# Non-local attention on one core: the first projections leave ScalarE ahead of the exponential's table, g and the result's shift go behind the first scores

## What is computed

```python
g     = (einsum('bchw,oc->bhwo', x, w_g) + b_g).reshape(B, N, Ci)
theta = (einsum('bchw,oc->bhwo', x, w_theta) + b_theta).reshape(B, N, Ci)
phi   = (einsum('bchw,oc->bohw', x, w_phi) + b_phi[:, None, None]).reshape(B, Ci, N)
att   = softmax(einsum('bnc,bcm->bnm', theta, phi), axis=-1)
y     = einsum('bnm,bmc->bnc', att, g).reshape(B, H, W, Ci)
out   = einsum('bhwc,oc->bohw', y, w_out) + b_out[:, None, None]
inv   = bn_gamma / sqrt(bn_var + BN_EPS)
out   = out * inv[:, None, None] + (bn_beta - bn_mean * inv)[:, None, None]
return x + out
```

## Time and profile before

| | us |
|---|---|
| median of three runs | 212.36 |
| lowest, highest | 211.96, 212.52 |
| the profiled execution: device time | 212.18 |
| its span, first to last instruction | 210.40 |
| TensorE busy (94% of the span) | 198.5 |
| VectorE busy (85%) | 178.4 |
| GpSimd busy (72%) | 152.4 |
| ScalarE busy (65%) | 136.8 |

### The profile page before, as it was taken

How to read it: one execution, slowest core, us unless ns; L and a number is a source line. 1 busy time by engine, 2 the same in 40 slices (tenths; PEclk the granted TensorE clock), 3 DMA queues, 4 the chain that set the end, 5 groups by cost and what they waited for, 6 DMA issues and landing times.

```text
span 210.4 us, 3966 instructions
## 1 busy us (share of the span) xinstructions
PE 198.5 (94%) x1100; PEld 130.9 (62%) x1100; DVE 178.4 (85%) x291; ACT 136.8 (65%) x245; POOL 152.4 (72%) x127
## 2 busy tenths in 40 slices
PE   7996989999999998999999999999999998999993
PEld 6585856586565856577555955667565854566542
DVE  0789899978998799978999599978999699989871
ACT  2776866758575847767577666756578575658721
POOL 2448898699669998699778998699887964774400
PEclk9999999999999999999999999999999999999999
DMA  5215967999999998899959995899977997786111
GB/s 156 88 60 154 212 126 155 229 215 168 230 106 247 229 183 167 165 249 232 189 129 259 220 200 133 190 252 216 153 160 167 224 170 166 134 108 114 50 37 66
DMA packets 59500, 35.28 MB, mean 168 GB/s; under 512 B 50400, under 2 KB 50912, under 8 KB 59488
## 3 DMA queue, kind: packets, MB, share of 16 engines
q1 hardware_dynamic: 59200, 35.01, 81.2%
q10 hardware_dynamic: 288, 0.14, 0.2%
HBM read 8.36 MB, written 4.23 MB: 60 GB/s over the span
## 4 chain that ended last, share of the span: by engine, by line
PE 58%; DVE 15%; ACT 12%; issue 10%; DMA 2%; ACTq 1%; DVEq 0%
PE ps_scores L721 17%; PE ps_y L733 11%; PE ps_flip L786 9%; ACT probs L544 8%; PE ps_misc L705 6%; DVE neg_max L586 6%; DVE pt_lo L686 5%; PE ps_y L740 5%; ACT pt_hi L532 4%; PE ps_misc L747 3%; PE ps_misc L811 3%; DVE y_norm L603 2%; PE ps_scores L759 2%; DMA w_tp<-w_tp_t_dram 2%; PE ps_flip L705 1%
## 5 line engine op out<-in xcount | busy, mean ns | idle before, releaser
L544 ACT ACTIVATE probs<-ps_scores,neg_max 128x1024 f32<-128x1024 f32 x64 | 71.7, 1120 | 32.3 <-DVE neg_max L591 23.4
L586 DVE TENSOR_REDUCE neg_max<-ps_scores 128x1 f32<-128x1024 f32 x64 | 77.8, 1216 | 0.9 <-PE ps_scores L721 0.9
L686 DVE SCALAR_TENSOR_TENSOR pt_lo<-ps_flip,pt_hi 128x512 f16<-128x512 f32 x84 | 54.0, 685 | 15.8 <-ACT pt_hi L532 15.6
L532 ACT ACTIVATE pt_hi<-ps_flip 128x512 f16<-128x512 f32 x84 | 45.7, 596 | 20.4 <-PE ps_flip L786 20.1
L721 PE MATMUL ps_scores<-phi_hh,theta_hl 128*128 128x512 f32 x128 | 45.8, 439 | 5.2 <-ACT probs L544 4.8
L426 POOL TENSOR_TENSOR p_lo<-probs,p_hi 128x1024 f16<-128x1024 f32 x22 | 47.1, 2141 | 4.3 <-POOL p_hi L422 2.6
L786 PE MATMUL ps_flip<-ident,probs 128*128 128x128 f32 x336 | 45.0, 276 | 1.0 <-ACT probs L544 0.6
L786 PEld LDWEIGHTS ps_flip<-ident,probs 128*128 128x128 f32 x336 | 37.2, 142 | 11.6 <-issue 5.7
L721 PE MATMUL ps_scores<-phi_ll,theta_hl 128*128 128x512 f32 x128 | 40.1, 394 | 0.0
L422 POOL TENSOR_SCALAR p_hi<-probs 128x1024 f16<-128x1024 f32 x22 | 23.6, 1071 | 11.3 <-ACT probs L544 8.3
L721 PEld LDWEIGHTS ps_scores<-phi_hh,theta_hl 128*128 128x128 f32 x128 | 19.3, 190 | 18.9 <-ACT probs L544 17.5
(11 more groups left out here) (80 smaller groups left out, 176.8 us busy)
## 6 DMA issues: line engine op xcount, KB each, us to landing
x_in<-x_in_dram SPq DMA_DIRECT2D x16, 256.0 KB, 3.3
inv_all<-inv_row SPq DMA_DIRECT2D x15, 256.0 KB, 4.1
out_dram<-resid SPq DMA_DIRECT2D x15, 256.0 KB, 2.7
phi_hh<-hi SPq DMA_DIRECT2D x14, 256.0 KB, 5.2
phi_ll<-lo SPq DMA_DIRECT2D x14, 256.0 KB, 5.7
theta_hl<-hi SPq DMA_DIRECT2D x7, 256.0 KB, 4.3
theta_hl<-lo SPq DMA_DIRECT2D x7, 256.0 KB, 5.1
pt_hi<-p_hi SPq DMA_TRANSPOSE x22, 4.5
```

What stands on the lines that cost most here:

```text
L532: nc.scalar.activation(pt_hi[ring][:, c * HALF_TILES:(c + 1) * HALF_TILES, slot * P:(slot + 1) * P], ps_flip[c][:, :].rearrange("p (a n) - ...
L544: nc.scalar.activation(probs[k % PROB_RING][:, :], ps_scores[k % 2][:, :], ACT.Exp, bias=neg_max[:, k % STEPS:k % STEPS + 1], accum_out=ro ...
L586: nc.vector.tensor_reduce(out=top, in_=ps_scores[k % 2][:, :], op=ALU.max, axis=AX.X, negate=True).then_inc(row_max_ready if by_dma(it, k) ...
L686: nc.vector.scalar_tensor_tensor(out=pt_lo[ring][where], in0=ps_flip[c][:, :].rearrange("p (a n) -> p a n", n=P), scalar=PROB_SCALE, in1=p ...
```

## The change

On ScalarE the exponential on `table_probe`, and with it the load of its table, goes from ahead of the five first Identities to behind them; it stays ahead of the evacuation of g. On TensorE the scores of tile 0 go ahead of the first half of g, and the second half of g with the small bias matmul and its wait for `w_out_in` goes into step 0, behind the scores of tile 1. On VectorE the two operations of the shift go behind the row maximum of tile 1, as a function called in step 0. Nothing is added or left out.

```diff
--- before.py
+++ after.py
@@ -497,14 +497,13 @@
             act.wait_ge(bn_step, 1)
             nc.scalar.activation(STD, VAR_EPS, ACT.Sqrt).then_inc(bn_std, 1)
 
-            act.wait_ge(bn_std, 1)
-            nc.scalar.activation(table_probe[:, :], STD, ACT.Exp)
-
             for n, (is_phi, cols, projected) in enumerate(first_order):
                 target, bias = ((theta_hl[0], BIAS_TT), (phi_hh[0], BIAS_PP))[is_phi]
                 act.wait_ge(first_proj, n + 1)
                 nc.scalar.activation(target[:, cols], projected, ACT.Identity,
                                      bias=bias).then_inc(first_hi, 1)
+            act.wait_ge(bn_std, 1)
+            nc.scalar.activation(table_probe[:, :], STD, ACT.Exp)
             act.wait_ge(g_ready, 1)
             evacuate_g(0, ps_flip[0][:, :], g_raw[0][:, :, :].rearrange("p t c -> p (t c)"))
 
@@ -606,12 +605,14 @@
                     in1=inv_all[half][:, :].rearrange("c (p t) -> c t p", t=HALF_TILES),
                     op0=ALU.mult, op1=ALU.mult).then_inc(y_scaled, 1)
 
+            def shift_of_result():
+                dve.wait_ge(g_bias_ready, 1)
+                nc.vector.tensor_tensor(BIAS_SUM, ps_flip[1][:, 0:1], B_OUT, ALU.add).then_inc(bn_step, 1)
+                dve.wait_ge(bn_step, 6)
+                nc.vector.scalar_tensor_tensor(out=SHIFT, in0=BIAS_SUM, scalar=INV, in1=BETA_SHIFT,
+                                               op0=ALU.mult, op1=ALU.add).then_inc(shift_ready, 1)
+
             row_maximum(0, 0)
-            dve.wait_ge(g_bias_ready, 1)
-            nc.vector.tensor_tensor(BIAS_SUM, ps_flip[1][:, 0:1], B_OUT, ALU.add).then_inc(bn_step, 1)
-            dve.wait_ge(bn_step, 6)
-            nc.vector.scalar_tensor_tensor(out=SHIFT, in0=BIAS_SUM, scalar=INV, in1=BETA_SHIFT,
-                                           op0=ALU.mult, op1=ALU.add).then_inc(shift_ready, 1)
 
             def step(it, k):
                 image, j = image_at(it, k), k % MT
@@ -690,6 +691,8 @@
                 t = tile_at(it, k + 1)
                 if exists(t, TILES):
                     row_maximum(it, k + 1)
+                if tile_is(it, k, 0):
+                    shift_of_result()
 
             run_steps(dve, step)
             dve.wait_ge(resid_ready, B)
@@ -758,13 +761,9 @@
                 pe.wait_ge(x_arrived[0][cols.start // BANK], 16)
                 nc.tensor.matmul(projected, w_tp[:, 2 * CI * is_phi:2 * CI * (is_phi + 1)],
                                  x_in[0][:, cols], start=True, stop=True).then_inc(first_proj, 1)
+            scores(0, 0, 0)
             pe.wait_ge(w_g_in, 16)
             project_g(ps_flip[0], 0, range(MT // 2))
-            scores(0, 0, 0)
-            project_g(ps_flip[0], 0, range(MT // 2, MT)).then_inc(g_ready, 1)
-            pe.wait_ge(w_out_in, 32)
-            nc.tensor.matmul(ps_flip[1][:, 0:1], wout[0:CI, 0:C], wout[0:CI, C:C + 1],
-                             start=True, stop=True).then_inc(g_bias_ready, 1)
             pe.wait_ge(ident_ready, 1)
 
             def step(it, k):
@@ -791,7 +790,11 @@
                 t = tile_at(it, k + 1)
                 if exists(t, TILES):
                     scores(t, it, k + 1)
-
+                if tile_is(it, k, 0):
+                    project_g(ps_flip[0], 0, range(MT // 2, MT)).then_inc(g_ready, 1)
+                    pe.wait_ge(w_out_in, 32)
+                    nc.tensor.matmul(ps_flip[1][:, 0:1], wout[0:CI, 0:C], wout[0:CI, C:C + 1],
+                                     start=True, stop=True).then_inc(g_bias_ready, 1)
 
                 image, j = image_at(it, k), k % MT
                 more = exists(image + 1, B)
```

## The result

The changed kernel takes 213.06 us in the median of 11 runs (212.38 to 213.58), the kernel before beside it 212.22 (211.90 to 212.77). The ratio is 1.0034, with a 95% interval of 1.0018 to 1.0050: slower by some 0.7 us (0.84 between the medians), where 0.88 was forecast. The profiled execution of the changed kernel took 212.56 us (span 210.7), that of the kernel before 212.18.

A forecast was written before the change was run, and what follows sets the result against it. It took the chain through TensorE, VectorE and ScalarE as the bound, with 2% DMA. Tile 2's maximum, at 15.77 instead of 14.89, adds 0.88 to 212.36: 213.24, range 212.4 to 213.8.

The forecast's parts named there:

- The hold: ScalarE's queue: g's evacuation, now released behind tile 1's scores, delays tile 0's exponential by 1.27, to 13.30.
- The table: ScalarE: exponential's table load moves behind the Identities, hidden by the wait for g; first scores 0.61 earlier.
- Rival 3: ScalarE's Identities still need a table load ahead of them: +1.16, 213.52; chance 0.13, shared with later GpSimd and ScalarE bounds.
- What is late at tile 3 is late at the end: VectorE's delay from tile 2, +0.88, carries through to the end because each queue keeps its fixed order.
- Rival 2: Later stages of the chain partly take up the delay; if half, +0.44 and 212.80; chance 0.15.
- The term of 0.61: TensorE's first scores start at 8.88 instead of 9.49, released by the third low part.
- the signs of being wrong: g's evacuation before 12, tile 2's delay smaller by the end, or a TensorE row below 13 us of another length.
- Rival 1: ScalarE is not held by g, so tile 2's maximum starts at 14.75: -0.14, 212.22; chance 0.10.

The follow-up runs named there:

- fastest kernel: Changed kernel with g evacuated behind tile 0's exponential and the first image's qk projections and evacuations moved later: 210.57 us, ratio 0.9926 to the kernel before.

## Why the prediction was right

**The hold, right.** The exponential of tile 0 was to start 13.30 - 8.88 = 4.42 behind the first scores; it did so by 4.38 (12.77 - 8.39). Tile 2's maximum was to start 6.89 behind them; it was 6.87 in all three profiles with g behind the scores and its evacuation ahead of the exponential. That it is the order of ScalarE's queue is shown by the kernel with the evacuation moved: 6.00.

**The table, right in its mechanism.** No load stands ahead of the Identities; the load of 1.28 at 9.07 and the probe are over at 10.57, and the wait for g to 12.28 covers them. Rival 3, which had Identity need its own load, falls. Its place came out when that load was put there by hand (first scores at 9.17, 9.16 forecast), and its price nearly: 1.16 above the kernel before was forecast, the ratio of 1.0063 gives 1.3. The drain of 1.38 of the Trainium skill's page "ScalarE: Activation LUTs" (section "What ACT_TABLE_LOAD costs") does not show here either: the load ends at 10.35, the next activation starts at 10.37, so the measurement decides against it for this place.

**What is late at tile 3 is late at the end, right.** Rival 2, a delay partly taken up later, falls by the last column of the table. What the prediction left out is small: `g_parts` behind `hi` adds 0.07 from tile 2 to tile 3 (3.91 against 3.84), so that tile 3 comes 10.78 behind the first scores against the forecast 15.77 + 3.84 - 8.88 = 10.73.

**Mis-sized: how much earlier the first scores come.** The term of 0.61 (9.49 to 8.88) rests on one execution, in which the projections ended at 8.84, later than in any of the other eight profiles (7.87 to 8.33). I treated that end as given. It moves from run to run, with the time at which TensorE's clock rises (last section). With the scores ahead of g and the table behind the Identities the first scores came between 8.06 and 8.42, held by the low parts behind the transfer of `vec` or, where the projections were later, by the second phi projection; those of the kernel before wait for its low part at 9.11 or 9.26 even when TensorE is early. From the two profiles of each, the gain is 9.49 - 8.39 = 1.10 and 9.31 - 8.06 = 1.25. At tile 3 the loss is 0.44 and 0.25 in these pairs. Where the projections end at 8.84 in both, I estimate it at 0.95, from first scores 0.65 behind that end in the one and 0.06 in the other. The ratio's 0.7 lies between, so I infer that many of the timed runs had a later end than most profiles; then that the 0.88 came so near is in part luck, since the one profile behind it had the latest end of the nine.

A run without a profile doesn't show its prologue, but its mean granted clock over the span is on record. In eight of the nine profiles the clock falls the later at the end, behind TensorE's last work, the later it rose (4.28 and 209.07 in the second profile of the kernel before, 6.17 and 210.97 in its first), and only a fall inside the span brings the mean below 1. Of the 11 runs of the changed kernel the five below 1 took 212.38 to 213.06, the six at 1 took 212.57 to 213.58; with all of g ahead of the scores of tile 1, six took 211.60 to 211.98 and six 212.27 to 213.04. That speaks for the inference and doesn't show it. It fits that the kernel before ran from 211.75 to 212.77, but for one run of 213.50, and the changed one from 212.29 to 213.58.

For the same reason two of the signs of being wrong came up: the first projections' rows were shorter (3.62 and 3.38 against 4.10), and in the second profile g's evacuation came at 11.95, ahead of 12. Behind the first scores it came by 3.89 in both profiles, where 12.81 - 8.88 = 3.93 was forecast.

**Rival 1's price, wrong.** With ScalarE not held I gave -0.14 and no measurable loss. The kernel that does this was 0.2% slower than before. The price stopped at tile 2: its maximum started 0.13 later there than I had worked out (6.00 against 14.75 - 8.88 = 5.87), and from tile 2 to tile 3 it took 4.12 where it had been 3.84, because VectorE's `g_parts` waits for GpSimd's `hi`. With both, -0.14 becomes +0.27, which the measured interval (0.1 to 0.7 us) takes in.

## What to carry to other kernels

When work is moved behind a step on one engine, look at what else that work's semaphore holds: an engine that evacuates it in queue order holds everything queued behind the evacuation, so move the evacuation with it. Before costing a gain in a prologue, take two or three profiles: a row that the change waits for may move from run to run, here with the clock's rise, while the kernel before waits for something else, and the gain moves with the difference. And where the remaining time equals a start plus a constant in every variant, that start is the thing to work on; here it led from a loss of 0.3% to a gain of 0.7%.

## What the runs showed of the hardware

A VectorE operation from SBUF to SBUF can stand still while GpSimd works. In the profile of the kernel before, a TENSOR_SCALAR on two elements per partition ended with GpSimd's operation, not by its own length:

```profile
32.16 1.05 POOL L422 TENSOR_SCALAR p_hi<-probs 128x1024 f16<-128x1024 f32 x1 [0.72 <-ACT probs L544]
32.32 0.91 DVE L631 TENSOR_SCALAR inv_sum<-inv_sum 128x2 f32<-128x2 f32 x1
```

It took 0.91; on one element per partition, at 21.84, with GpSimd already 0.26 into a tensor-tensor operation, the same line took 0.15, so not every pair blocks. In the fastest kernel the second `g_parts` operation, which reads two SBUF tensors, took 1.65 beside GpSimd's `lo`; in the kernel before it started 0.08 ahead of GpSimd's `p_hi`, took 0.74 itself, and `p_hi` took 1.56 in place of the usual 1.07. The Trainium skill, "SBUF — State Buffer", section "SBUF: two separate sides", calls the port pair that VectorE and GpSimd share an exclusive lock, held for a whole instruction, with the other fully blocked; the 0.91, the 1.65 with the 1.56, and the 0.28 behind `hi` agree with it. Why one element went through was not tried.

The same first matmuls on TensorE are spaced differently from run to run: in the first profile of the kernel before, the passes of 512 columns start 0.85 and 0.72 apart at first and 0.43 later, in the second 0.43 from the beginning. The clock record that the traces keep goes with it: it begins, at the full level (2.4 GHz), at 6.17 us in the first profile and at 4.28 in the second. In the first profile of the changed kernel it begins at 5.17, and there one pass of 512 columns is 0.66 from the next and the following ones 0.43; in the remaining six it begins at 4.05 to 4.73, and the passes are some 0.43 apart throughout. Ahead of these times no level is recorded, and the granted-clock column of the profile reads 1.00 there only for want of a record; that it is the lower level (1.2 GHz) is inferred from the spacing of 0.85, twice 0.43. TensorE had been at matmuls since 1.05 in every profile, so an earlier start doesn't set the profiles apart. Between the two late ones, the end of the projections moves by about half of what the rise does (8.84 against 8.33 for 6.17 against 5.17).
